# Window attention on one core: where TensorE weighs the values, behind the next pair's maxima or in front of the additions

## The chip, the cores and the metric

One core of a Trainium2 chip runs the whole kernel. The metric is the device time of one execution in microseconds (us), as the median of the runs shown. A core has five engines with a queue of instructions each, which are worked off in order: TensorE (PE, its weight loads are PEld), VectorE (DVE), ScalarE (ACT), GpSimd (POOL) and SyncE (SP, which issues most transfers). They wait for each other by semaphores.

## The reference

x has 8 samples of 32 x 32 positions with 256 channels. Two stages run over it:

```
x = x + attention(groupnorm(x))      # windows of 8 x 8, 16 heads of 16, bias by relative position, shift mask
x = x + lif(groupnorm(x))            # a linear layer, then spikes of leaky neurons over the 8 samples
attention: scores = (q * 0.25) @ k.T + bias + mask ; softmax over the keys ; out = softmax @ v
```

The group norm has 32 groups of 8 channels, with mean and variance over all positions of a sample.

## The kernel before

**Tiling.** The channels lie on the partitions. A sample is four rows of four windows; a row has 256 positions. The attention works on *pairs*: two windows of one row, 64 in all (n from 0 to 63), with k = n mod 8 as place in the sample and p = n mod 2. An even pair is the left half of a row, an odd pair the right half. Every engine runs a function `pair(n, row, k, s)` 64 times, and the order of instructions on each engine is the order in which that function is written; nothing reorders it but the semaphores' waits.

**What one pair needs.** q, k and v of a row are made by TensorE from the normalised row, split into a high and a low part (three products each): `project_q` and `project_k` in odd pairs for the row after next, `project_v` in even pairs for the next row. ScalarE and VectorE copy them out of PSUM as a high and a low half precision part (`q_high`, `k_high`, `v_high`, and `q_low`, `k_low`, `v_low`). SyncE moves q and k into stacks by twelve transfers for a row (`move_q_and_k`). Then, for pair n:

- `max_scores`: TensorE computes the scores once with the queries on the partitions (`max_ps`), VectorE takes the negative maximum over the keys (`maxima`).
- `turn_maxima`: TensorE transposes these, ScalarE copies them to `max_rows` (line 606).
- `scores`: TensorE computes the scores again with the keys on the partitions (`score_ps`, one buffer of two banks): 32 products (line 1023), 8 products that add the biases (line 1032), then a wait for `max_rows`, and 16 products that add the maxima (line 1039). All of these are matmuls on quarters of the array (64 x 64 tiles), four at a time.
- ScalarE takes the exponential twice for each half of the heads, to single precision (`probs`, line 615) and to half precision (`p_hi`, line 616). GpSimd takes the difference (`p_lo`, line 447).
- `weigh_values`: TensorE multiplies the exponentials by the values, 24 matmuls on the full array (line 1065) into `pv_ps`, which has one buffer of two banks. It waits for both halves of `p_lo`, in odd pairs for `v_lo`, and for `attn_done` of the pair before, because VectorE must have read `pv_ps`.
- VectorE divides by the sums (`attention_out`, line 814), TensorE transposes (`turn_attention`, line 1075), ScalarE copies (line 579), GpSimd adds to x (line 433).

The stages overlap: in pair n TensorE computes the scores of n, the maxima of n + 1, the values of n - 1, and turns the attention of n - 2. `project_q` writes the bank that v was in, and so waits until VectorE has read v (`v_lo_done`).

**Norms beside the pairs.** The norm of a later sample is worked out in some pairs (`norm_beside`). Its group means are two small matmuls, `average_means` (line 922, stage 0, pair k = 6, and pair 0), its variances `average_variances` (line 926, stage 1, k = 7; pair 1; pair 60 for the last norm). Both are called from `weigh_values` as `beside`, ahead of its matmuls, and wait for VectorE's moments (line 683) or spreads. VectorE works on the variances (line 704) ahead of dividing the attention. The last norm's roots are GpSimd's, ahead of the `p_lo` of pair 61.

After the pairs, the second stage (LIF) runs over 32 units, one after the other.

Line numbers are those of the kernel before.

Of the kernel before, what the change touches and what calls it, by code (L numbers as in the profile page):

```python
# [6 lines left out]
def swin_attention_then_lif_kernel(nc, image, x, qkv_w, qkv_b, bias_table, lif_w, lif_b, out):  # L7
# [40 lines left out]
    with ctx:  # L48
# [154 lines left out]
        def is_first(n, lag):  # L203

            return isinstance(n, int) and n < lag
# [32 lines left out]
        def is_last_pair(n):  # L238

            return isinstance(n, int) and n == PAIRS - 1  # L240
# [12 lines left out]
        BODY = 2 * WROWS  # L253
# [663 lines left out]
        def _(pe):  # L917
# [6 lines left out]
            def average_variances(norm, width, averages):  # L924
                pe.wait_ge(norm_dve, norm * NORM_STEPS + 4)
                pe.matmul(averages[:, NORMS:NORMS + width], group_avg[:, :], tiny[2][:, 0:width], start=True, stop=True)\
                  .then_inc(norm_pe, 1)
# [84 lines left out]
                                             start=False, stop=(w == 1 and m == 1 and h == 1))  # L1012
                last.then_inc(max_ps_done, 1)

            def scores(n, row, k):

                slot, p = k // 2 % 2, k % 2
                for g, w in itertools.product(range(QUADS), range(2)):
                    col = (2 * g + w) * WS
                    for h, e in itertools.product(range(HALVES), range(2)):  # L1020
                        at = h * WCOLS + 2 * p + w
                        rows = stacks_of[e ^ h]
                        pe.matmul(score_ps[halves[e], h, col:col + WS], k_stack[slot][rows, g, at, :], q_stack[slot][rows, g, at, :],
                                  start=(g == 0 and w == 0), stop=False)
                first, last_variant = variant(k, 0), variant(k, 1)
                for part in range(2):
                    for h, e in itertools.product(range(HALVES), range(2)):
                        rows = halves[e ^ h]
                        biases = bias_s[rows, part, first:last_variant + 1, h, :, :].rearrange("p v g i -> p g v i")
                        if last_variant == first:  # L1030
                            biases = biases.to_broadcast([WS, QUADS, 2, WS])
                        pe.matmul(score_ps[halves[e], h, :].rearrange("p (g w i) -> p g w i", g=QUADS, w=2), flip[rows, :], biases,
                                  start=False, stop=False)
                pe.wait_ge(max_rows_done, n + 1)
                for w, m in itertools.product(range(2), range(2)):
                    for h, e in itertools.product(range(HALVES), range(2)):
                        rows = halves[e ^ h]
                        dst = score_ps[halves[e], h, :].rearrange("p (m q w i) -> p m w q i", m=2, q=2, w=2)[:, m, w, :, :]
                        last = pe.matmul(dst, pick_max[rows, (2 * w + m) * 2 + h, :],  # L1039
                                         max_rows[p][rows, :].rearrange("p (q i) -> p q i", q=2),  # L1040
                                         start=False, stop=(w == 1 and m == 1))
                        if w == 1 and m == 1 and e == 1:
                            last.then_inc(score_ps_done, 1)
# [51 lines left out]
            def pair(n, row, k, s):  # L1095
                p = k % 2
                if p == 0 and not is_last_row(row):
                    project_v((k // 2 + 1) % 2, row + 1)
                elif p == 1 and not is_last_row(row, 2):
                    project_q(k // 2 % 2, row + 2)  # L1100
                    project_k(k // 2 % 2, row + 2, n - 2)
                if is_first(n, 8):
                    pe.wait_ge(bias_lo_done, variant(k, 1) + 1)
                following = (n + 1, row + 1 if p else row, (k + 1) % BODY)

                wait(pe, p_hi_done, n * 2)
                turn_maxima(n)
                scores(n, row, k)
                norm, _, width, stage = norm_beside(s, k)
                beside = None  # L1110
                if stage == 0:
                    beside = lambda: average_means(norm, width, spare_averages)
                if stage == 1:
                    beside = lambda: average_variances(norm, width, spare_averages)
                if not is_last_pair(n):
                    await_max_operands(*following)
                    max_scores(following[2])
                if not is_first(n, 1):
                    weigh_values(n - 1, row if p else row - 1, (k - 1) % BODY, beside)
                elif beside:  # L1120
                    beside()
                if p == 1 and not is_last_row(row, 2):
                    pe.wait_ge(k_lo_done, row + 3)
                if not is_first(n, 2):
                    turn_attention(n - 2, p)
                if is_last_pair(n):
                    unit_products(0, 0)
# [54 lines left out]
```

## Time and profile before

| | us |
|---|---|
| runs shown (3) | 482.02, 482.65, 490.40 |
| median | 482.65 |
| profiled execution, its own time | 487.65 |
| its span, first to last instruction | 485.80 |

| engine | busy us | share of the span |
|---|---|---|
| TensorE matmuls | 412.3 | 85% |
| TensorE weight loads | 346.8 | 71% |
| VectorE | 401.1 | 83% |
| ScalarE | 381.5 | 79% |
| GpSimd | 279.5 | 58% |

The shares are means over a start (to about 85 us), the steady stretch of pairs (to about 390), the last pairs (to about 415) and the second stage. Times in the rows below are us from the first instruction. A row of the timeline has its start, its length, the engine, the line, the operation, what it writes and reads with sizes, how often it stands there merged, and in brackets the idle time of its engine before it with what ended that.

### The profile page before, as it was taken

How to read it: one execution, taken by the hardware profiler on the slowest of the kernel's cores; microseconds unless marked ns; L12 is line 12 of the kernel's file. 1: busy time of each engine (PE TensorE's matmuls, PEld its weight loads, DVE VectorE, ACT ScalarE, POOL GpSimd, SP SyncE). 2: the span in 40 equal slices, each digit the busy share in tenths (PEclk: the TensorE clock that was granted, in tenths of full speed). 3: DMA queues.
4: the chain of work that ended last, by engine and by line, in shares of the span. 5: the costliest groups of instructions: out<-in, count | busy, mean ns of one | idle time of the engine just before them, and what ended most of it. 6: DMA issues, size and time to landing. Idle time of an engine off the chain costs nothing.

```text
span 485.8 us, 22209 instructions
## 1 busy us (share of the span) xinstructions
PE 412.3 (85%) x9320; PEld 346.8 (71%) x9320; DVE 401.1 (83%) x872; ACT 381.5 (79%) x913; POOL 279.5 (58%) x392
## 2 busy tenths in 40 slices
PE   0476768999999999999989997999799886799996
PEld 0465657777777777787777786878677775588885
DVE  6767995998898889889889995988687875689887
ACT  3377897999998889999989995999798866546550
POOL 5625786786667557767866693669565558400000
PEclk9987998999999999999999997999999988899999
DMA  6422221233333232332323323122212220133333
GB/s 210 137 82 72 90 69 61 85 98 97 96 98 94 89 111 92 102 95 94 107 89 98 95 92 104 49 72 68 84 63 74 68 70 3 43 123 124 143 133 131
DMA packets 42488, 44.98 MB, mean 93 GB/s; under 512 B 8082, under 2 KB 33940, under 8 KB 42388
## 3 DMA queue, kind: packets, MB, share of 16 engines
q1 hardware_dynamic: 41632, 43.55, 27.0%
q8 instruction: 74, 1.21, 1.1%
q14 instruction: 26, 0.21, 0.1%
q10 hardware_dynamic: 756, 0.01, 0.1%
HBM read 9.97 MB, written 8.39 MB: 38 GB/s over the span
## 4 chain that ended last, share of the span: by engine, by line
PE 44%; SPq 15%; ACT 14%; DVE 11%; DMA 7%; issue 5%; POOL 3%; ACTq 0%; DVEq 0%; POOLq 0%
SPq L320 15%; PE proj_ps L950 5%; PE pv_ps L1065 5%; DMA k_stack<-k_flat 5%; PE proj_ps L952 4%; PE proj_ps L951 4%; ACT k_flat L514 3%; ACT v_hi L531 3%; PE score_ps L939 3%; PE score_ps L1039 3%; PE proj_ps L939 3%; PE pv_ps L939 3%; PE max_ps L939 2%; DVE v_lo L793 2%; ACT max_rows L606 2%
## 5 line engine op out<-in xcount | busy, mean ns | idle before, releaser
L447 POOL TENSOR_TENSOR p_lo<-probs,p_hi 128x512 f16<-128x512 f32 x128 | 146.5, 1166 | 109.3 <-ACT p_hi L616 87.0
L799 DVE TENSOR_REDUCE neg_max<-max_ps 128x16 f16<-128x1024 f32 x64 | 78.3, 1223 | 20.9 <-PE max_ps L1010 19.9
L615 ACT ACTIVATE probs<-score_ps 128x512 f32<-128x512 f32 x128 | 76.9, 601 | 22.9 <-PE score_ps L1039 18.7
L950 PE MATMUL proj_ps<-xn_hi,w_hi 128*128 128x256 f32 x256 | 79.4, 310 | 17.8 <-POOL xn_lo L400 11.8
L616 ACT ACTIVATE p_hi<-score_ps 128x512 f16<-128x512 f32 x128 | 77.2, 603 | 0.0
L951 PE MATMUL proj_ps<-xn_lo,w_hi 128*128 128x256 f32 x256 | 74.2, 290 | 0.0
L952 PE MATMUL proj_ps<-xn_hi,w_lo 128*128 128x256 f32 x256 | 74.0, 289 | 0.0
L793 DVE TENSOR_TENSOR v_lo<-proj_ps,v_hi 64x256 f16<-64x256 f32 x128 | 54.2, 423 | 20.3 <-ACT v_hi L531 18.8
L950 PEld LDWEIGHTS proj_ps<-xn_hi,w_hi 128*128 128x128 f32 x256 | 51.2, 200 | 23.2 <-issue 16.4
L1065 PE MATMUL pv_ps<-v_hi,p_hi 128*128 128x68 f16 x512 | 56.3, 198 | 3.0 <-POOL p_lo L447 3.0
L531 ACT ACTIVATE v_hi<-proj_ps 64x256 f16<-64x256 f32 x128 | 50.5, 394 | 10.0 <-PE proj_ps L962 8.3
L814 DVE TENSOR_TENSOR attn<-pv_ps,recip 64x256 f32<-64x256 f32 x128 | 54.0, 422 | 3.0
L1065 PE MATMUL pv_ps<-v_lo,p_hi 128*128 128x68 f16 x512 | 56.1, 195 | 0.0
L1065 PE MATMUL pv_ps<-v_hi,p_lo 128*128 128x68 f16 x512 | 55.8, 196 | 0.0
L1065 PEld LDWEIGHTS pv_ps<-v_hi,p_hi 128*128 128x128 f16 x512 | 49.3, 101 | 5.5 <-POOL p_lo L447 3.5
L1039 PEld LDWEIGHTS score_ps<-max_rows,pick_max 64*64 64x64 f16 x1024 | 16.8, 106 | 49.9 <-ACT max_rows L606 49.3
L951 PEld LDWEIGHTS proj_ps<-xn_lo,w_hi 128*128 128x128 f32 x256 | 51.3, 200 | 0.0
L952 PEld LDWEIGHTS proj_ps<-xn_hi,w_lo 128*128 128x128 f32 x256 | 51.2, 200 | 0.0
L433 POOL TENSOR_TENSOR xc<-xc,attn_cm 128x256 f32<-128x256 f32 x64 | 47.2, 738 | 6.5 <-ACT attn_cm L579 6.5
L661 DVE BATCH_NORM_STATS2 x_stats<-xc 128x6 f32<-128x256 f32 x128 | 47.4, 416 | 3.7 <-DMA xc<-in_x_dram 2.7
L579 ACT ACTIVATE attn_cm<-proj_ps,b_cols 128x128 f32<-128x128 f32 x128 | 41.3, 389 | 10.3 <-PE proj_ps L1075 10.2
L1065 PEld LDWEIGHTS pv_ps<-v_lo,p_hi 128*128 128x128 f16 x512 | 49.0, 100 | 0.2 <-issue 0.2
(129 smaller groups left out, 1142.7 us busy)
## 6 DMA issues: line engine op xcount, KB each, us to landing
q_stack<-q_flat SPq DMA_DIRECT2D x192, 64.0 KB
k_stack<-k_flat SPq DMA_DIRECT2D x192, 64.0 KB
xc<-in_x_dram SPq DMA_DIRECT2D x32, 256.0 KB, 3.4
out_dram<-xc SPq DMA_DIRECT2D x32, 256.0 KB, 2.4
w_raw<-in_qkv_w_dram SPq DMA_DIRECT2D x1, 768.0 KB, 6.5
bias_raw<-in_bias_table_dram SPq DMA_DIRECT2D x16, 32.0 KB
w_lif<-in_lif_w_dram SPq DMA_DIRECT2D x1, 256.0 KB, 4.6
b_cols<-in_qkv_b_dram ACTq DMA_DIRECT2D x4, 0.2 KB
```

Source lines behind the costliest of these rows:

```text
L320: sp.dma_start(stacks[slot][first:first + D, :, :, :].rearrange("d g n i -> d g (n i)"), flat[slot][r * WS:(r + 1) * WS, part, :])\
L447: pool.tensor_tensor(p_lo[p][:, quads, :, :].rearrange("p g w i -> p (g w i)"), probs[:, quads, :, :].rearrange("p g w i -> p (g w i)"), p ...
L531: last = act.activation(v_block(v_hi[slot], w, e), v_part(w, e), ACT.Copy)
L615: act.activation(probs[:, quads, :, :].rearrange("p g w i -> p (g w i)"), score_ps[:, h, :], ACT.Exp)
L616: act.activation(p_hi[p][:, quads, :, :].rearrange("p g w i -> p (g w i)"), score_ps[:, h, :], ACT.Exp)\
L793: last = dve.tensor_tensor(v_block(v_lo[slot], w, e), v_part(w, e), v_block(v_hi[slot], w, e), ALU.subtract)
L799: dve.tensor_reduce(neg_max[:, :].rearrange("p (m n) -> p m n", m=2)[:, :, 0:8], max_ps[:, :, :].rearrange("p m (n j) -> p m n j", j=WS), ...
L814: last = dve.tensor_tensor(attn[k % 2][rows, :, :, :], heads[rows, :, w, :, 0:D], recip[rows, :, w, :].unsqueeze(3).to_broadcast([WS, HALV ...
L950: pe.matmul(dst, w_hi[:, c, cols], high[:, tok], start=(c == 0), stop=False)
L951: pe.matmul(dst, w_hi[:, c, cols], low[:, tok], start=False, stop=False)
L952: last = pe.matmul(dst, w_lo[:, c, cols], high[:, tok], start=False, stop=(c == HALVES - 1))
L1065: last = pe.matmul(cols[:, :, g, :], pp[p][:, h * QUADS + g, :, :].rearrange("p w i -> p (w i)"), vv[k // 2][:, p, h * QUADS + g, :, :, :] ...
```

## The change

In even pairs the call of `weigh_values` (or of `beside` alone, where there are no values, as in pair 0) moves into `scores`, between the bias products and the wait for `max_rows`. In odd pairs it stays behind `max_scores`. Nothing else is changed.

```diff
-            def scores(n, row, k):
+            def scores(n, row, k, values=None):
...
                         pe.matmul(score_ps[halves[e], h, :].rearrange("p (g w i) -> p g w i", g=QUADS, w=2), flip[rows, :], biases,
                                   start=False, stop=False)
+                if values:
+                    values()
                 pe.wait_ge(max_rows_done, n + 1)
...
                 turn_maxima(n)
-                scores(n, row, k)
                 norm, _, width, stage = norm_beside(s, k)
                 beside = None
                 if stage == 0:
                     beside = lambda: average_means(norm, width, spare_averages)
                 if stage == 1:
                     beside = lambda: average_variances(norm, width, spare_averages)
+
+                def values():
+                    if not is_first(n, 1):
+                        weigh_values(n - 1, row if p else row - 1, (k - 1) % BODY, beside)
+                    elif beside:
+                        beside()
+
+                scores(n, row, k, None if p else values)
                 if not is_last_pair(n):
                     await_max_operands(*following)
                     max_scores(following[2])
-                if not is_first(n, 1):
-                    weigh_values(n - 1, row if p else row - 1, (k - 1) % BODY, beside)
-                elif beside:
-                    beside()
+                if p:
+                    values()
```

## Rows read from the trace of the kernel before

**Rows 1.** Windows, 85 to 390: us, then busy us (instructions) of each engine, clock.

```profile
85.00:390.00 305.00, 278.82 (x7452) 231.43 (x7452) 262.86 (x581) 273.42 (x666) 207.51 (x266) 0.99 0.28 89
```

**Rows 2.** Waits, 85 to 390: who waited for whom, us, times, longest.

```profile
ACT probs L615 <- PE score_ps L1039: 16.1, 27, 0.9
...
PE max_ps L1003 <- DMA k_stack<-k_flat: 8.1, 10, 2.2
```

**Rows 3.** Timeline of TensorE in pair 18, a plain even pair.

```profile
151.12 0.42 PE L1023 MATMUL score_ps<-q_stack,k_stack 48*64 48x64 f16 x32
151.37 0.63 PE L1032 MATMUL score_ps<-bias_s,flip 64*64 64x512 f16 x8
152.32 0.42 PE L1039 MATMUL score_ps<-max_rows,pick_max 64*64 64x128 f16 x16 [0.31 <-ACT max_rows L606]
...
152.78 0.42 PE L1010 MATMUL max_ps<-k_stack,q_stack 48*64 48x64 f16 x32
153.14 0.20 PE L1065 MATMUL pv_ps<-v_hi,p_hi 128*128 128x68 f16 x1
...
153.90 0.41 PE L1075 MATMUL proj_ps<-ident,attn 128*128 128x128 f32 x2
154.15 0.36 PE L950 MATMUL proj_ps<-xn_hi,w_hi 128*128 128x256 f32 x1
```

**Rows 4.** Timeline of VectorE in pair 18.

```profile
150.86 0.86 DVE L814 TENSOR_TENSOR attn<-pv_ps,recip 64x256 f32<-64x256 f32 x2
...
153.14 0.87 DVE L793 TENSOR_TENSOR v_lo<-proj_ps,v_hi 64x256 f16<-64x256 f32 x2 [0.29 <-ACT v_hi L531]
```

**Rows 5.** Timeline of ScalarE in pair 18: the second copy of v, the exponential.

```profile
152.29 0.81 ACT L531 ACTIVATE v_hi<-proj_ps 64x256 f16<-64x256 f32 x2
153.13 0.60 ACT L615 ACTIVATE probs<-score_ps 128x512 f32<-128x512 f32 x1
```

**Rows 6.** Timeline of all engines in pair 14, with a norm's means.

```profile
128.99 0.39 DVE L683 BATCH_NORM_AGGREGATE moments<-x_stats 128x2 f32<-128x24 f32 x2
...
130.24 0.60 ACT L615 ACTIVATE probs<-score_ps 128x512 f32<-128x512 f32 x1
130.25 0.38 PE L922 MATMUL pv_ps<-moments,group_avg 128*128 128x2 f32 x2
...
130.49 0.19 PE L1065 MATMUL pv_ps<-v_hi,p_hi 128*128 128x68 f16 x1
```

**Rows 7.** Timeline of VectorE and ScalarE in pair 46, with a norm's means.

```profile
312.58 0.39 DVE L683 BATCH_NORM_AGGREGATE moments<-x_stats 128x2 f32<-128x24 f32 x2
...
313.87 0.60 ACT L615 ACTIVATE probs<-score_ps 128x512 f32<-128x512 f32 x1
```

**Rows 8.** Timeline of VectorE and ScalarE in pair 8, after a norm's variances.

```profile
95.21 0.86 DVE L814 TENSOR_TENSOR attn<-pv_ps,recip 64x256 f32<-64x256 f32 x2
...
96.49 0.60 ACT L615 ACTIVATE probs<-score_ps 128x512 f32<-128x512 f32 x1
```

**Rows 9.** Timeline of VectorE and ScalarE in pair 40, after a norm's variances.

```profile
275.07 0.86 DVE L814 TENSOR_TENSOR attn<-pv_ps,recip 64x256 f32<-64x256 f32 x2
...
276.69 0.60 ACT L615 ACTIVATE probs<-score_ps 128x512 f32<-128x512 f32 x1
```

**Rows 10.** Timeline of all engines in pair 0.

```profile
37.96 0.60 ACT L615 ACTIVATE probs<-score_ps 128x512 f32<-128x512 f32 x1
...
39.06 0.39 DVE L683 BATCH_NORM_AGGREGATE moments<-x_stats 128x2 f32<-128x24 f32 x2
...
41.90 0.64 PE L1003 MATMUL max_ps<-bias_q,ident_h 64*64 64x512 f16 x4 [4.19 <-ACT bias_q L541]
...
42.90 0.59 PE L922 MATMUL pv_ps<-moments,group_avg 128*128 128x2 f32 x2
```

**Rows 11.** Timeline of GpSimd (p_lo of pair 61) and ScalarE (pair 62).

```profile
403.98 2.26 POOL L447 TENSOR_TENSOR p_lo<-probs,p_hi 128x512 f16<-128x512 f32 x2
...
405.21 0.60 ACT L615 ACTIVATE probs<-score_ps 128x512 f32<-128x512 f32 x1 [2.76 <-POOL p_lo L447]
```

## The prediction

> **What bounds the kernel now.** I read the busy shares of the stretch in which all pairs look alike, then the list of waits, then single pairs in order of time. In that stretch ScalarE works 273.42 of 305.00 us, nine tenths, VectorE 262.86, and TensorE shows 278.82 of matmuls whose spans overlap [rows 1]. Of ScalarE's 31.6 us of idle time 16.1 lie in 27 waits of 0.60 us each for the additions of the maxima, and these stand in odd pairs, where nothing lies between the copy of the maxima and the exponentials [rows 2]. TensorE in turn waits for the copy of the maxima in front of its additions, 0.31 us in pair 18 [rows 3]: this is the hole that the values would now lie in.
>
> Pair 18 is an even pair without anything special. The products of its scores start at 151.12, the bias products at 151.37; these run until 152.00, and TensorE then stands until the additions at 152.32 [rows 3]. The additions, the next pair's maxima (152.78), the product of values (153.14 to 153.90), the turning of the attention and the projection of q (154.15) follow without a gap [rows 3]. Two rows say who really sets the pace there. The exponential starts at 153.13, 0.81 us after the additions began and not 0.6 as in odd pairs, so it came when ScalarE was done with the second copy of v, not when the scores were done [rows 3, 5]. And v_lo ends on VectorE at 153.14 + 0.87 = 154.01, 0.14 us before q's projection begins: that projection may not overwrite v's bank before it [rows 3, 4]. So in an even pair TensorE's end is tied to v_lo and ScalarE's start to its own queue; an earlier end of TensorE's block has no taker.
>
> **The change part by part.** In the 31 even pairs from 2 on, the 24 matmuls of the values of pair n-1 move in front of the additions of pair n. Their number stays the same, and TensorE's is the only queue in which anything changes place, and no transfer is issued from it. Four waits move with them to the head of TensorE's queue: for p_lo of pair n-1 (GpSimd), for attn of pair n-2 (VectorE, which must have read the bank), in some pairs for the moments of a norm (VectorE) together with the two small matmuls that average them, and, being an in-order queue, all that stood behind: additions, maxima of n+1, the turning, the projection. For the additions wait the exponentials, and with them ScalarE.
>
> *Plain even pairs.* The bias matmuls end at 152.00 by the row; a matmul's row overlaps the next one by about 0.17 (0.20 long at a spacing of 0.03), so TensorE can take new work at about 151.83 [rows 3]. attn of pair 16 is done at 150.86 + 0.86 = 151.72 [rows 4], and a handover of 0.1 (an estimate, under the 0.14 from v_lo to the projection) makes 151.82: just in time. Going from 64x64 tiles to full ones costs something: 32 products of the scores take 0.25 to the next line (151.12 to 151.37), 32 of the same size in front of the values 0.36 (152.78 to 153.14), so I take 0.10 for the switch [rows 3]. For the way back no row stands alone; between 0 and 0.10, I take 0.05. The value block takes 0.76. Additions then begin at 151.83 + 0.10 + 0.76 + 0.05 = 152.74 instead of 152.32, the exponential can start 0.55 later (0.60 of the odd pairs' wait less the handover), 153.29 against 153.13: +0.16. The cover of ScalarE's second v copy swallows the most, not quite all. Maxima of n+1 end some 0.4 later, still before VectorE has done v_lo.
>
> The Trainium skill, in TensorEngine Tiling (Array Packing), Key Properties, says that changing the tiling mode, not just the tile, drains the TensorE. That speaks against this change, since an even pair now goes 64, 128, 64, 128 where it went 64, 128. The row's 0.11 agrees that there is a price, though it shows one direction; if there were none, the plain pairs would cost nothing and the sum would be about 2.5 us less.
>
> Of the 20 or so plain pairs most are followed by some slack (below); I count 1.0 us for all, between 0 and 20 x 0.16 = 3.2.
>
> *Pairs with a norm's means in them* (seventh pair of a sample: 14, 22, 30, 38, 46; pair 6 has ScalarE so late that it costs nothing). VectorE finishes the moments only at 128.99 + 0.39 = 129.38, 0.89 us after pair 14's bias products began; today TensorE asks for them at 130.25, when they are long there [rows 6]. Now: 129.38 + 0.10 handover + 0.24 for the two small matmuls (130.25 to 130.49) + 0.10 + 0.76 + 0.05 + 0.55 = 131.18 for the exponential that started at 130.24: +0.94 [rows 6]. In pair 46, the last, 312.58 + 0.39 + 1.80 = 314.77 against 313.87: +0.90 [rows 7]. Five pairs, 4.6 us.
>
> *Pairs after a norm's variances* (first pair of a sample: 8, 16, 24, 32, 40). VectorE did the variances ahead of attn, which is then late: in pair 8 at 95.21 + 0.86 = 96.07, plus 1.56 (the terms above without the small matmuls) 97.63 against 96.49: +1.14 [rows 8]; in pair 40 275.93 + 1.56 = 277.49 against 276.69: +0.80 [rows 9]. Five pairs between these, 4.9 us.
>
> Together 9.5. ScalarE goes from an even pair's exponentials to the next odd pair's without idle time but the 0.6, so the delay travels on. Where the odd pair then finds TensorE waiting for the moved keys, the delay uses up that wait: there are 10 such waits, 8.1 us, four of them (1.4 us of the 8.1, read along the timeline) behind these ten pairs [rows 2]. For short waits of ScalarE in the odd pairs I take off another 0.9, an estimate whose lower end is nothing. 9.5 - 2.3 = 7.2.
>
> *Pair 0* has no values, but the means of a norm go in front of its additions. Their moments end at 39.06 + 0.39 = 39.45, while the exponential started at 37.96 [rows 10]. 39.45 + 0.10 + 0.45 (the two small matmuls' 0.59 less their tail) + 0.05 + 0.55 = 40.60: +2.6. The maxima of pair 1 wait for a bias table that ScalarE makes behind these exponentials (41.90), so they go with it, and q's projection with them; the means' 0.59 between the two is gone [rows 10]. I take 2.1, between 2.0 and 2.6.
>
> *Pair 62.* GpSimd, held by the last norm's roots, ends p_lo of pair 61 at 403.98 + 2.26 = 406.24 [rows 11]. Today the scores are ready by then and the exponential starts at 405.21, on p_lo's first half [rows 11]. Now the additions stand behind the values, which need both halves: 406.24 + 0.10 + 0.10 + 0.76 + 0.05 + 0.55 = 407.80, +2.6; ScalarE saves about 0.2 of a later wait. 2.4, all of it on the way into the second stage, which nothing shortens.
>
> Sum: 1.0 + 7.2 + 2.1 + 2.4 = 12.7 us. The profiled execution took 487.65 us (span 485.80), so it would be 500.35; the median of the runs shown is 482.65, 5.0 lower, and 12.7 above that is **495.4 us**.
>
> **The rivals.** *TensorE is the bound (faster).* It shows the longest busy time [rows 1] and stands before the additions in nearly every pair. If v_lo did not hold q's projection, an even pair would win the standing time less two switches, 152.32 - 151.83 - 0.15 = 0.34; times 31 that is 10.5 us: 472. Against it stand v_lo's 0.14 and ScalarE's nine tenths. It decides if v_lo is done well before TensorE comes to the projection, which the rows do not show.
> The Trainium skill, in Perfetto Trace Analysis, Identifying the Most-Contended Engine, holds matmul busy time for a poor measure and wants weight loads counted; these are 231.43 us here [rows 1], so by that rule TensorE is not the most contended, as I forecast.
>
> *The queue of moved keys sets the pace (no measurable change).* A row of windows waits for the stacks of q and k, and ScalarE's path is bypassed where that wait ends last. If the ten delays all fall into such waits, outside this one execution or because the transfers start as early as before, only pair 0 and pair 62 remain: 2.1 + 2.4 = 4.5 us, 487.2. For it: ten such waits, of up to 2.2 us [rows 2]. Against: six of the ten pairs have none behind them, and the transfers of a row start after the odd pair's additions, which are themselves late.
>
> *Nothing is absorbed (slower still).* If the waits for keys stay as long as they are, all of 9.5 + 3.2 + 2.1 + 2.6 = 17.4 counts: 500.1.
>
> *No effect*: the waits now at the head are all met in time, as in pair 18, in every pair. The rows of pairs 0, 8, 14 and 62 exclude it for any run in which VectorE keeps its order.
>
> **How the numbers follow.** Two per cent, about what a measurement of this kernel tells from no change, is 9.65 us: 492.3. Chances: forecast 0.60 (its own range 491 to 498, a tenth of it below 492.3), nothing absorbed 0.13, keys set the pace 0.20, TensorE bound 0.04, no effect 0.03. Slower by over 2%: 0.54 + 0.13 = 0.67; within: 0.06 + 0.20 + 0.03 = 0.29; faster: 0.04. The range goes from the keys' 487 to 501, a little above nothing absorbed, for the way back between tile sizes at its upper bound.
>
> **What would show it.** In the profile after: TensorE's wait for the copy of the maxima nearly gone; in its place waits of the value block for attn, moments and, once, p_lo; in pair 18 the exponential within 0.2 us of the end of the second v copy; in pairs like 14 and 8 ScalarE idle for about 0.9 us in front of the exponentials; pair 0's additions at about 40; pair 62's exponential at 2.6 us more behind its p_lo. Wrong would be: q's projection starting clearly earlier behind v's projection, or waits for the keys shrinking by as much as the delays add.

## The result and the profile after

The changed kernel takes 499.19 us (median of four runs, 495.59 to 500.72) against 484.63 for the kernel before beside it (482.02 to 490.4): a ratio of 1.031, with an interval of 1.021 to 1.041. It is slower. The median lies 3.8 us above the forecast and within its range; the difference of the medians is 14.6 us where 12.7 were forecast. The execution that was profiled took 499.86 us with a span of 498.1, which is 12.3 more than the span of before. From L1034 on, line numbers are two higher than in the listing: the additions are now L1041, the values L1067.

Windows of the kernel after, its steady stretch, columns as in [rows 1]:

```profile
85.00:400.00 315.00, 284.93 (x7529) 234.57 (x7530) 267.84 (x583) 274.01 (x672) 210.68 (x271) 0.99 0.27 87
```

I cut the stretch ten us longer than in [rows 1] so that it holds about the same instructions (7529 matmuls for 7452, 672 of ScalarE for 666). ScalarE has worked 274.01 us in it where it had 273.42: what came is waiting. The list of waits of the same stretch (who waited for whom, us, times, longest) shows where:

```profile
ACT probs L615 <- PE score_ps L1041: 30.9, 53, 1.1
PEld score_ps L1041 <- ACT max_rows L606: 19.5, 28, 0.7
...
PEld pv_ps L1067 <- POOL p_lo L447: 6.9, 13, 0.8
...
PE pv_ps L1067 <- DVE attn L814: 4.1, 5, 0.9
PE pv_ps L922 <- DVE moments L683: 4.0, 7, 1.5
...
PE max_ps L1003 <- DMA k_stack<-k_flat: 3.4, 7, 0.8
```

ScalarE waits for the additions 53 times instead of 27, 30.9 us instead of 16.1 [rows 2]: the even pairs have joined the odd ones. Weight loads wait for the copy of the maxima in 28 cases only, 27 of them in odd pairs; in the even pairs the waits for p_lo, attn and the moments have taken its place. The waits of matmuls for the moved keys are down from 8.1 us to 3.4 [rows 2].

Pair 18, the plain even pair, in the timeline of the kernel after:

```profile
156.75 0.86 DVE L814 TENSOR_TENSOR attn<-pv_ps,recip 64x256 f32<-64x256 f32 x2
157.13 0.63 PE L1032 MATMUL score_ps<-bias_s,flip 64*64 64x512 f16 x8
157.76 0.19 PE L1067 MATMUL pv_ps<-v_hi,p_hi 128*128 128x68 f16 x1
158.04 0.81 ACT L531 ACTIVATE v_hi<-proj_ps 64x256 f16<-64x256 f32 x2
158.48 0.19 PE L1067 MATMUL pv_ps<-v_hi,p_lo 128*128 128x68 f16 x1
158.60 0.42 PE L1041 MATMUL score_ps<-max_rows,pick_max 64*64 64x128 f16 x16
158.88 0.87 DVE L793 TENSOR_TENSOR v_lo<-proj_ps,v_hi 64x256 f16<-64x256 f32 x2 [0.28 <-ACT v_hi L531]
159.14 0.60 ACT L615 ACTIVATE probs<-score_ps 128x512 f32<-128x512 f32 x1 [0.29 <-PE score_ps L1041]
159.90 0.35 PE L950 MATMUL proj_ps<-xn_hi,w_hi 128*128 128x256 f32 x1
```

The additions start 1.47 us after the bias products where it was 0.95 [rows 3]; the second copy of v ends at 158.85, and ScalarE now stands for 0.29 us where the copy used to hide the additions [rows 5]. v_lo still ends 0.15 before q's projection begins (159.75, 159.90), as before: the end of TensorE's block was not brought forward.

The special pairs in the same timeline: pair 0 (from 37.96), pair 8 (97.86), pair 14 (133.49), pair 26 (204.58) and pair 62 (413.37):

```profile
37.96 0.39 DVE L683 BATCH_NORM_AGGREGATE moments<-x_stats 128x2 f32<-128x24 f32 x2
38.40 0.58 PE L922 MATMUL pv_ps<-moments,group_avg 128*128 128x2 f32 x2 [2.01 <-DVE moments L683]
39.59 0.60 ACT L615 ACTIVATE probs<-score_ps 128x512 f32<-128x512 f32 x1 [2.50 <-PE score_ps L1041]
...
97.86 1.16 DVE L704 TENSOR_SCALAR root_guess<-tiny 128x2 int32<-128x2 int32 x1
...
99.30 0.86 DVE L814 TENSOR_TENSOR attn<-pv_ps,recip 64x256 f32<-64x256 f32 x2
100.31 0.19 PE L1067 MATMUL pv_ps<-v_hi,p_hi 128*128 128x68 f16 x1 [0.85 <-DVE attn L814]
101.68 0.60 ACT L615 ACTIVATE probs<-score_ps 128x512 f32<-128x512 f32 x1 [1.14 <-PE score_ps L1041]
...
133.49 0.39 DVE L683 BATCH_NORM_AGGREGATE moments<-x_stats 128x2 f32<-128x24 f32 x2
134.02 0.35 PE L922 MATMUL pv_ps<-moments,group_avg 128*128 128x2 f32 x2 [0.41 <-DVE moments L683]
135.61 0.60 ACT L615 ACTIVATE probs<-score_ps 128x512 f32<-128x512 f32 x1 [0.87 <-PE score_ps L1041]
...
204.58 0.20 PE L1067 MATMUL pv_ps<-v_hi,p_hi 128*128 128x68 f16 x1 [0.30 <-POOL p_lo L447]
205.97 0.60 ACT L615 ACTIVATE probs<-score_ps 128x512 f32<-128x512 f32 x1 [0.56 <-PE score_ps L1041]
...
413.37 2.26 POOL L447 TENSOR_TENSOR p_lo<-probs,p_hi 128x512 f16<-128x512 f32 x2
415.69 0.24 PE L1067 MATMUL pv_ps<-v_hi,p_hi 128*128 128x68 f16 x1 [3.44 <-POOL p_lo L447]
417.15 0.64 PE L1041 MATMUL score_ps<-max_rows,pick_max 64*64 64x128 f16 x16
417.91 0.60 ACT L615 ACTIVATE probs<-score_ps 128x512 f32<-128x512 f32 x1 [6.06 <-PE score_ps L1041]
```

In each of them TensorE's first value (or average) names the engine that it waited for, and ScalarE's first exponential names the additions: the chain that was forecast. Two distances are new. In pair 26 p_lo is late, which no term of the sum had. In pair 62 the additions begin 1.46 us after the first value, where pair 18 needs 0.84; its value block runs at half the clock (windows, below).

### The profile page after: what moved, and what is told of

Read it like the earlier page. It is cut to its first block, busy times and chain, and to the rows that moved or that the text cites. A ratio compares the mean times of both kernels' runs of the same rounds, so it can differ in the third digit from the quotient of the medians.

```text
span 498.1 us, 22209 instructions
## 1 busy us (share of the span) xinstructions
PE 418.3 (84%) x9320; PEld 348.6 (70%) x9320; DVE 404.9 (81%) x872; ACT 379.1 (76%) x913; POOL 279.1 (56%) x392
## 4 chain that ended last, share of the span: by engine, by line
PE 38%; DVE 14%; ACT 14%; SPq 12%; issue 8%; POOL 8%; DMA 5%; ACTq 0%; DVEq 0%; POOLq 0%
SPq L320 12%; PE pv_ps L1067 6%; POOL p_lo L447 4%; DMA k_stack<-k_flat 4%; ACT p_hi L616 3%; PE score_ps L1041 3%; PE proj_ps L950 3%; PE score_ps L939 3%; ACT k_flat L514 3%; PE proj_ps L939 3%; PE pv_ps L939 3%; DVE x_stats L661 3%; PE proj_ps L952 2%; PE proj_ps L951 2%; PE max_ps L939 2%
## 5 line engine op out<-in xcount | busy, mean ns | idle before, releaser
L950 PE MATMUL proj_ps<-xn_hi,w_hi 128*128 128x256 f32 x256 | 80.7, 315 | 27.3 <-DVE w_lo L752 8.7
L1067 PEld LDWEIGHTS pv_ps<-v_hi,p_hi 128*128 128x128 f16 x512 | 49.4, 101 | 21.8 <-POOL p_lo L447 11.7
L1067 PE MATMUL pv_ps<-v_hi,p_hi 128*128 128x68 f16 x512 | 56.0, 197 | 9.8 <-DVE attn L814 5.1
L1067 PE MATMUL pv_ps<-v_lo,p_hi 128*128 128x68 f16 x512 | 55.8, 195 | 0.0
L1067 PE MATMUL pv_ps<-v_hi,p_lo 128*128 128x68 f16 x512 | 55.5, 196 | 0.0
L1067 PEld LDWEIGHTS pv_ps<-v_hi,p_lo 128*128 128x128 f16 x512 | 49.0, 98 | 0.0
L1067 PEld LDWEIGHTS pv_ps<-v_lo,p_hi 128*128 128x128 f16 x512 | 48.9, 100 | 0.0
L492 ACT ACTIVATE unit<-xc,shift,rstd 128x256 f32<-128x256 f32 x64 | 34.0, 594 | 16.0 <-PE score_ps L939 8.1
```

The lines of the kernel that those rows point to most:

```text
L950: pe.matmul(dst, w_hi[:, c, cols], high[:, tok], start=(c == 0), stop=False)
L1067: last = pe.matmul(cols[:, :, g, :], pp[p][:, h * QUADS + g, :, :].rearrange("p w i -> p (w i)"), vv[k // 2][:, p, h * QUADS + g, :, :, :] ...
```

## The experiments

**Theory**: the values, and what they wait for, put off the additions; ScalarE's exponentials then start later than its second copy of v would let them, and the delay goes through to the end. **Rival 1**: TensorE is the bound, and the two further switches of tile size per even pair are what costs. **Rival 2**: the waits themselves cost, at whichever place they lock an engine. **Rival 3**: only the norm pairs, or only pairs 0 and 62, carry the loss. Later runs ask whether the waiting can be bought back.

The table is worked out along the timelines: the mean time from the turning of the maxima to the first exponential of the pair, in us, by position of the pair in its sample (first, seventh, third, fifth pair), then the waits of weight loads for moved keys in pairs 9 to 59 (they begin earlier than the matmuls' waits of [rows 2] and are longer), the steady stretch from pair 9's first exponential to pair 57's, and the span of the profiled execution. Each line is one execution.

```
kernel             first  seventh  third  fifth  keys  steady  span
before             2.06   2.08     2.08   2.06   10.4  274.0   485.8
after              3.13   2.93     2.49   2.30    5.0  277.5   498.1
values_second      2.05   2.07     2.08   2.07   10.5  271.6   484.1
waits_only         2.14   2.07     2.09   2.07   10.2  273.0   483.5
plain_only         2.06   2.07     2.49   2.29    8.0  274.2   485.3
norms_only         3.17   2.93     2.09   2.12    7.0  275.2   487.4
norms_root_means   2.42   2.30     2.08   2.06    6.9  271.8   483.2
ends_only          2.05   2.07     2.08   2.10   10.0  273.0   490.0
ends_behind        3.15   2.93     2.48   2.29    4.0  277.2   493.1
mended             2.34   2.30     2.47   2.26    8.6  275.5   489.9
before_again       2.06   2.07     2.08   2.07   10.4  274.0   487.5
```

TensorE's granted clock was 0.5 for some us of the steady stretch in before, before_again, waits_only, plain_only and ends_only, and 1.0 throughout in the other six. Of those, values_second has pairs like those of before; so its 271.6 us is the fair measure for the steady stretch of the others among the six.

**values_second.** The values go one step back, behind the additions but still in front of the next maxima. The number of switches per pair stays that of the change.

```diff
-                scores(n, row, k, None if p else values)
+                scores(n, row, k)
+                if not p:
+                    values()
```

> In even pairs the additions stay first and the values come right behind them, ahead of the next pair's maxima: as many changes of tile size as in the changed kernel, but no wait and no work in front of the additions. Theory (the cost is the exponentials' delay by what now stands in front of the additions; ScalarE's queue sets the pace): the loss is gone, 0 to +1 per cent against the kernel before, and pair 62 costs nothing. Rival (the values' earlier place costs TensorE itself, by the two further switches between tile sizes and by waits at the head of its queue): most of the changed kernel's +3 per cent stays. If TensorE were the bound, nothing is won either, as it still stands for the copy of the maxima.

Measured: 1.003 (0.999 to 1.008). The loss is gone. Its pair 18 in the timeline:

```profile
152.03 0.81 ACT L531 ACTIVATE v_hi<-proj_ps 64x256 f16<-64x256 f32 x2
152.06 0.42 PE L1041 MATMUL score_ps<-max_rows,pick_max 64*64 64x128 f16 x16 [0.31 <-ACT max_rows L606]
...
152.41 0.20 PE L1067 MATMUL pv_ps<-v_hi,p_hi 128*128 128x68 f16 x1
...
152.87 0.60 ACT L615 ACTIVATE probs<-score_ps 128x512 f32<-128x512 f32 x1
```

The exponential again follows the copy of v without idle time. Rival 1 falls as to its price: the extra switches cost nothing that is seen. Whether TensorE is the bound is left to q_short, since TensorE still stands for the copy of the maxima here. What costs is the place of the values, with their waits, ahead of the additions.

**waits_only.** Only the waits of the values (for p_lo, attn and the norm's step) go in front of the additions, in the even pairs from 2 to 60; the matmuls stay where they were.

```diff
+                def waits():
+                    pe.wait_ge(p_lo_done, n * 2)
+                    wait(pe, attn_done, n - 1)
+                    if stage in (0, 1):
+                        pe.wait_ge(norm_dve, norm * NORM_STEPS + (1, 4)[stage])
...
-                scores(n, row, k, None if p else values)
+                scores(n, row, k, waits if p == 0 and 0 < n < 62 else None)
...
-                if p:
-                    values()
+                values()
```

> TensorE's order of matmuls as in the kernel before, but in the 30 even pairs between the ends the value block's waits (for p_lo, attention and, where there is a norm, moments) stand in front of the wait for the copy of the maxima, without its matmuls. Theory (a wait and the 0.8 us of work behind it exceed the 0.8 us by which ScalarE is late only together): pairs like 8 lose 0.2 to 0.3 us, all others nothing, the waits for keys take it up: ratio 1.00 to 1.003. Rival (the waits alone are the price): +5 to +7 us, 1.010 to 1.015.

Measured: 0.999 (0.994 to 1.003). Pair 8 in its timeline, the pair with the latest attn:

```profile
96.33 0.42 PE L1041 MATMUL score_ps<-max_rows,pick_max 64*64 64x128 f16 x16 [0.80 <-DVE attn L814]
...
96.86 0.60 ACT L615 ACTIVATE probs<-score_ps 128x512 f32<-128x512 f32 x1 [0.23 <-PE score_ps L1041]
```

TensorE waits 0.80 us for attn, and the exponential is 0.23 late, because the copy of v covers the rest; the mean of the first pairs rises by 0.08. So the waits alone fall too (rival 2). In the same pairs wait and block together cost 2.8 per cent (ends_behind, below), and wait and block behind the additions cost nothing that is seen (values_second). The block ahead of the additions without any wait was not run; the nearest to it are pairs whose waits are met almost in time, such as the fifth ones, which are 0.24 us late.

**plain_only, norms_only, ends_only.** The change in one class of pairs each; elsewhere the values stay behind.

```diff
-                scores(n, row, k, None if p else values)
+                front = k in (2, 4) and n < 60
+                scores(n, row, k, values if front else None)
...
-                if p:
+                if not front:
                     values()
```

In norms_only the condition is `k in (0, 6) and 8 <= n < 48`, in ends_only `n in (0, 62)`.

> The values in front of the additions only in the 15 even pairs without a norm's wait and away from both ends (third and fifth pair of each sample but the last's fifth). Theory: each of these pairs delays its exponentials by 0.2 us, or 0.5 in the third pair of a sample where p_lo is late; 5.4 us in sum, of which the waits for moved keys take more than half: +1 to +4 us, ratio 1.00 to 1.01. Rival (every pair pays alike by its order): 15 of 31 pairs, +7 us, ratio 1.015.

> The values in front of the additions only in the ten pairs 8, 14, 16, 22, ... 46 that stand beside or behind a norm's steps on VectorE. Theory: 0.9 us each in front of the exponentials, 9 us in sum, of which waits for moved keys take 1.5 to 3: +6 to +7.5 us, ratio 1.012 to 1.016. Rival (every pair pays alike): 10 of 31 pairs, +4 us, ratio 1.008; rival (the keys' queue sets the pace): +0 to +2 us.

> The values (in pair 0 the means) in front only in pairs 0 and 62. Theory: 2.0 to 2.9 us for pair 0 and 3.4 for pair 62, all on the path: ratio 1.011 to 1.013. Rival (the run with both put back gained less, so what follows takes most of it up): 1.00 to 1.005.

Measured: 1.012 (1.000 to 1.023), 1.016 (1.004 to 1.029) and 1.015 (1.007 to 1.024). The table says that plain pairs and norm pairs behave alone as they do in the whole change, to within 0.05 us; the way from the turning to the exponential in pair 62 is 6.61 us in ends_only as in the whole change (3.31 before). In each class the exponentials are late, which ends rival 3 as to the mechanism; as to the time, the interval of the plain pairs only just leaves out 1 (1.0004). The parts do not add up: the three ratios make 4.3 per cent where the whole has 3.1, and the spans of the three profiles only 5.3 us where the whole has 12.3. The intervals are 1.7 to 2.5 per cent wide, so these runs settle the mechanism in each pair but not its share of the time. The end in ends_only, GpSimd and ScalarE in the timeline:

```profile
405.25 2.26 POOL L447 TENSOR_TENSOR p_lo<-probs,p_hi 128x512 f16<-128x512 f32 x2
...
409.80 0.60 ACT L615 ACTIVATE probs<-score_ps 128x512 f32<-128x512 f32 x1 [6.06 <-PE score_ps L1041]
```

The exponential comes 409.80 - 407.51 = 2.29 us after p_lo, in the whole change 417.91 - 415.63 = 2.28, and in the kernel before it came 1.03 ahead of it [rows 11].

**ends_behind.** The complement: the change in all even pairs but 0 and 62 (`front = p == 0 and 0 < n < 62`).

> The changed kernel with pairs 0 and 62 put back to the order before. Theory: pair 0 gave 1.6 us and pair 62 3.4 us in the trace, both on the path; the sum of 5 us goes, ratio 1.018 to 1.023 where the changed kernel has 1.031. Rival (the ends' delays are taken up by the second stage or by what follows): stays at 1.03.

Measured: 1.028 (1.021 to 1.035), more than expected. In its trace pair 62 is as before (3.33 us from the turning to the exponential, 6.61 in the whole change, 3.31 before), and the way from pair 57's exponential to pair 63's is 33.53 us as against 37.34 in the change and 33.50 before. So 3.8 us are back at the end of the first stage, yet the ratio fell by 0.3 points only, well within its interval. The spans of the profiles do fit: ends_behind has 7.3 us more than before, ends_only 4.2, together 11.5 of the 12.3. Its start is as slow as the change's: 57.03 us from pair 1's exponential to pair 9's (56.73 in the change, 53.61 before).

**norms_root_means.** norms_only, with two things mended: the small matmuls for the means go behind the maxima again, and VectorE makes the roots' guess behind attn, not ahead of it.

```diff
-                        weigh_values(n - 1, row if p else row - 1, (k - 1) % BODY, beside)
+                        weigh_values(n - 1, row if p else row - 1, (k - 1) % BODY, beside if not front else None)
...
                 if not front:
                     values()
+                elif beside:
+                    beside()
...
+                if stage == 1:
+                    norm_guess(norm, width)
```

> The values in front only in the same ten pairs 8, 14, 16, ... 46 as in the run with these alone (ratio 1.016), but with what made them late moved out of the way: the small matmuls of the means stand behind the next maxima again, and VectorE makes the first guess of the roots behind the attention instead of ahead of it. Theory (the waits for moments and for a late attention are the price): each of the ten pairs falls from 0.9 us to 0.2 to 0.4, so +0 to +2 us, ratio 1.00 to 1.004. Rival (the place of the values itself is the price): unchanged at about 1.016.

Measured: 1.007 (1.004 to 1.011). VectorE in its pair 8:

```profile
94.86 0.86 DVE L817 TENSOR_TENSOR attn<-pv_ps,recip 64x256 f32<-64x256 f32 x2
95.75 0.56 DVE L706 TENSOR_SCALAR root_guess<-tiny 128x2 int32<-128x2 int32 x1
```

attn now comes first. The delay of the first pairs falls from 1.1 to 0.36 us and that of the seventh from 0.85 to 0.22, so both named causes are real. The steady stretch, 3.6 us over values_second in norms_only, hardly differs from it here; the ratio falls from 1.016 to 1.007, though the two intervals overlap. What is left of the delay has the size of a plain pair's, which I read as the value block itself.

**mended.** Both cures in all even pairs but 0 and 62.

> The changed kernel with pairs 0 and 62 as before, the small matmuls of the means behind the next maxima, and VectorE's first guess of the roots behind the attention: the values of 30 even pairs still stand in front of the additions, but the long waits are gone. Theory: 0.2 to 0.4 us is left for each pair, 8 us in sum, of which the waits for keys take 5, and up to 2 us for the clock at the start: ratio 1.005 to 1.012. Rival (the place of the values itself): stays at 1.02 to 1.03.

Measured: 1.017 (1.008 to 1.025), half a point above what was expected. The even pairs are late by 0.2 to 0.4 us each, as the table says, which costs 3.9 us of the steady stretch against values_second. Another 2.1 us are lost between pairs 2 and 3 (10.42 us against 8.33 in the kernel before). That the guess for a norm's roots now stands behind pair 1's attn does not explain them: norms_root_means has it there too and takes 8.40 us. TensorE's clock does (windows, columns as in [rows 1]):

```profile
57.20:64.00 6.80, 6.04 (x64) 5.84 (x68) 3.81 (x8) 3.80 (x11) 4.50 (x11) 0.50 0.22 68
```

The kernel before, in the profile of before_again, has the clock at 0.50 in the same projection and takes 9.84 us from pair 2 to pair 3, with nothing changed. No form of the change that keeps the values ahead of the additions beat the kernel before.

**q_short**, on the kernel before: q is projected from the high parts alone; the matmuls of the low parts are left out. If TensorE sets the pace, this must give time back.

```diff
-                project_channels(banks[6], 0, xn_hi[slot], xn_lo[slot]).then_inc(q_ps_done, 1)
+                for h in range(HALVES):
+                    for c in range(HALVES):
+                        last = pe.matmul(banks[6][:, h * ROWTOK:(h + 1) * ROWTOK], w_hi[:, c, h * 128:(h + 1) * 128],
+                                         xn_hi[slot][:, c * ROWTOK:(c + 1) * ROWTOK], start=(c == 0), stop=(c == HALVES - 1))
+                last.then_inc(q_ps_done, 1)
```

> The kernel before, its order unchanged, with q projected from the high parts alone (4 matmuls instead of 12 for a row; the low parts of q's projection are left out): TensorE has 8 x 0.117 = 0.94 us less work in each of 30 odd pairs. Theory (ScalarE's queue and the keys' transfers set the pace, TensorE's end is tied to others): 0 to -1 per cent. Rival (TensorE is the bound): -28 us, -6 per cent.

Measured: 0.988 (0.983 to 0.993). The waits of its steady stretch (85 to 395):

```profile
PEld proj_ps L950 <- ACT attn_cm L579: 26.2, 27, 1.1
...
ACT probs L615 <- PE score_ps L1043: 16.1, 27, 0.9
```

The same wait for attn_cm has 2.3 us in the kernel before. Most of what TensorE saves (0.94 us in each of 30 pairs), it now waits for ScalarE, and ScalarE's own wait is to the tenth what it was.

**xn_in_hole and v_early_xn**, on the kernel before, ask the opposite: whether filling ScalarE's 0.6 us in the odd pairs gives time back. xn_in_hole moves the high part of xn there; v_early_xn also moves v's projection to right behind the odd pairs' additions.

```diff
-                if p == 0 and not is_first(n, 1) and not is_last_row(row, 2):
-                    xn_high(k // 2 % 2, row + 3)
...
                     .then_inc(max_rows_done, 1)
+                if p == 1 and not is_last_row(row, 3):
+                    xn_high(nxt % 2, row + 4)
... (v_early_xn alone)
-                if p == 0 and not is_last_row(row):
-                    project_v((k // 2 + 1) % 2, row + 1)
+                if n == 0:
+                    project_v(1, 1)
...
+                if p == 1 and not is_last_row(row, 2):
+                    project_v(k // 2 % 2, row + 2)
```

> The kernel before with TensorE's order unchanged; ScalarE makes the high part of the normalised row in odd pairs between the copy of the maxima and the exponentials, where it stands idle for 0.6 us, instead of at the start of the next even pair (0.5 to 0.65 us). If ScalarE's queue alone sets the pace: 30 x 0.5 = -15 us, ratio 0.97. If ScalarE then waits for v's projection instead, which it does already in 13 even pairs of the stretch, and the keys' transfers hold their share: -2 to -6 us, ratio 0.988 to 0.996. If TensorE is the bound: 1.00.

> The same, and TensorE projects v in odd pairs right behind the additions of the maxima, not behind the turning of the attention at the start of the next even pair. Then neither the wait for moved keys nor the values stand in front of v's projection, and ScalarE finds v when it comes. Theory (ScalarE's queue is the bound, with v's projection and the keys next): -8 to -15 us, ratio 0.97 to 0.985, as the keys' wait is now filled with work. Rival (the later maxima of the next pair delay VectorE and the turned maxima by the projection's 1.5 us): no gain or up to +2 per cent.

Measured: 1.005 (1.000 to 1.009) and 1.057 (1.045 to 1.069). Both theories of ScalarE's queue missed; the first came out at what was written for TensorE as the bound. The waits of xn_in_hole, 85 to 395:

```profile
ACT v_hi L531 <- PE proj_ps L962: 16.1, 27, 1.2
...
ACT probs L615 <- PE score_ps L1039: 0.6, 1, 0.6
```

15.5 of the 16.1 us are filled, and 10.6 us open again one step on: the wait for v's projection was 5.5 us before. So at that step ScalarE waits for TensorE's order of work; that TensorE's amount of work is not the bound, q_short had shown. The steady stretch of this one profile is 268.2 us, 3.4 less than that of values_second, but the whole runs are not faster. Bringing that projection forward opened a third one, in v_early_xn's waits:

```profile
DVE neg_max L799 <- PE max_ps L1010: 51.3, 26, 2.1
...
ACT attn_cm L579 <- PE proj_ps L1075: 35.2, 28, 1.8
```

16.4 and 8.4 before. So ScalarE is not a bound in the sense that any idle time taken from it comes back. I read the pair as a closed loop through three engines, in which ScalarE's path is the longest way round by little.

**before_again.** One further profile of the kernel before, to see whether its long waits for keys belong to one execution.

> The kernel before once more, for one look: whether its two long waits for moved keys (2.4 us in pair 43, 2.1 us in pair 51) and the fall of TensorE's clock to its lower level behind the first belong to the kernel or to the one execution that was profiled. If to the execution: the waits for keys between pairs 9 and 59 fall from 10.7 us to 6 to 8, and the span from pair 9's to pair 57's exponential from 274.0 to about 270.

Measured: a span of 487.5 us, 10.4 us of waits for keys in pairs 9 to 59, and the same 274.0 us from pair 9 to pair 57. The longest stands at the same pair, here in the timeline of TensorE:

```profile
296.13 0.41 PE L1003 MATMUL max_ps<-bias_q,ident_h 64*64 64x512 f16 x4 [1.61 <-DMA k_stack<-k_flat]
```

In the first profile it has 2.20 us, at 295.50. These waits belong to the kernel and not to one execution. The fall of the clock behind the longest recurs as well, for a shorter stretch (0.51 from 296.90 to 300.40), and a further one to 0.50 from 344.70, where the first profile has 1.00. At the start the two executions of the one kernel differ by 1.5 us: from pair 1's exponential to pair 9's they take 53.61 and 55.09.

## Why the prediction came out as it did

**The mechanism held**, and each step of it can be seen. TensorE's wait for the copy of the maxima went in the even pairs, nothing took the time that was freed (v_lo holds q's projection by 0.15 us, as it did), and the exponentials wait for the additions. By the Trainium skill (Perfetto Trace Analysis, Identifying the Most-Contended Engine), TensorE's headroom is judged by its weight loads and the work done, not by matmul spans. q_short agrees, since fewer matmuls gave 1.2 per cent and mostly a wait.

**Plain pairs.** Forecast +0.16; measured +0.24 in fifth pairs, +0.41 in third ones, and +0.25 in pair 18, so that its exponential missed the 0.2 us behind the copy of v that were to show the forecast right. The value block starts 0.63 us after the bias products and not 0.56, being held by attn or p_lo, which end at 157.61 and 157.62. The way back from full tiles to 64x64 is 158.60 - 158.48 - 0.03 = 0.09, near the upper end of what I allowed. In third pairs GpSimd's p_lo comes late, as in pair 26: I had taken this wait to be met everywhere but in pair 62. By the Trainium skill, in TensorEngine Tiling (Array Packing), Key Properties, a change of tiling mode drains the TensorE. The rows agree that a change has a price, about 0.1 us each way, and in values_second it costs nothing that is seen where nobody waits behind it.

**Norm pairs.** In pair 14 the exponential comes 135.61 - 133.88 = 1.73 us after the moments (forecast 1.80), in pair 8 101.68 - 100.16 = 1.52 after attn (forecast 1.56). The means over five pairs are +0.85 and +1.07, within the forecast's 0.90 to 0.94 and 0.80 to 1.14 or just below. norms_root_means confirms both causes by taking them away. Pair 2, behind pair 1's variances, is of this kind too (late by 1.27 us); I had counted it with the plain ones.

**What was absorbed** is the first mis-sized term. I took off 1.4 us for waits for keys behind ten pairs, out of 8.1. In the two profiles these waits fell by 8.1 - 3.4 = 4.7 us, since plain pairs too run into them (in plain_only the weight loads' waits fall from 10.4 to 8.0). The delays themselves are larger too: from pair 10 to pair 56 the exponentials of the even pairs are late by 13.1 us in all, of which the nine norm pairs have 8.5, as forecast, and the plain ones 4.6, where I had counted 1.0 and at most 3.2. From pair 9's exponential to pair 57's the kernel lost only 3.55 us, where the forecast's parts for this stretch make about 7. A part of that is not the change's: in the kernel before, TensorE had half the clock around pair 43, which the kernel after lacks (windows of before; columns as in [rows 1]):

```profile
73.00:76.40 3.40, 3.40 (x18) 3.40 (x17) 1.06 (x3) 1.56 (x4) 2.00 (x3) 0.50 0.25 69
...
294.80:301.70 6.90, 6.21 (x114) 5.63 (x118) 2.99 (x6) 2.68 (x7) 4.24 (x4) 0.51 0.32 106
```

I read about 3 us of the stretch's difference from that second window, and this reading is an estimate. Against values_second, whose clock does not fall there, the kernel after lost 277.5 - 271.6 = 5.9 us; measured so, the net forecast of 7 is near, by two terms that were both too small and cancel.

**Pair 0** was sized well as a delay: the exponential comes 39.59 - 38.35 = 1.24 us after the moments (forecast 1.15), where it came 1.49 ahead of them before. Up to pair 1's exponential the kernel lost 1.8 us of span where I took 2.1, but this is not set apart from the start's own changes: runs with pair 0 as before reach that point anywhere from 48.58 us (plain_only) to 51.32 (ends_behind), the kernel after at 50.85.

**Pair 62** is the second mis-sized term: 2.28 us behind p_lo instead of 1.56, so 3.3 instead of 2.6, and 3.8 instead of 2.4 up to pair 63. The step that failed is the 0.76 for the value block with the 0.55 behind it: both were taken at the full clock. Windows of the kernel after:

```profile
72.10:78.90 6.80, 4.86 (x22) 4.86 (x23) 3.83 (x8) 4.32 (x12) 4.74 (x5) 0.50 0.21 60
...
89.10:92.50 3.40, 3.18 (x15) 3.19 (x16) 3.20 (x9) 2.00 (x6) 3.10 (x4) 0.51 0.41 128
413.40:423.60 10.20, 7.05 (x162) 5.23 (x163) 3.09 (x6) 4.88 (x12) 5.87 (x7) 0.50 0.02 4
```

From 413.40 on TensorE has 0.50 of its clock, the 1.2 GHz level. That lies within a stand of 3.44 us (412.25 to 415.69) in which it waited for p_lo.

**The start** is a term that was missing. From pair 1's exponential to pair 9's the kernel lost 3.1 us, of which pair 8's delay explains about one. Projections of pairs 4 to 7 run at 0.50 and 0.51 in two windows of together 10.2 us, where the kernel before has one of 3.4: pairs 4 to 5 take 0.67 us more, 6 to 7 take 1.52 more. How much of this is the change's is not shown. The kernel before itself takes 53.61 us in one profile and 55.09 in the other, in which the clock is low in one more place (windows of before_again):

```profile
58.00:61.40 3.40, 3.35 (x16) 3.38 (x17) 2.26 (x4) 1.30 (x4) 3.09 (x8) 0.50 0.37 109
```

Against the one the loss is 3.1 us, against the other 1.6. ends_behind has the same two windows as the change and takes 57.03 us; values_second, plain_only and norms_only take 53.55 to 53.89. That would fit a loss which comes with the values ahead in all of these pairs together, but with one profile each, and so large a difference between two profiles of one kernel, it is only argued.

So the stages make 1.8 + 3.1 + 3.55 + 3.8 + 0.0 (second stage) = 12.3 us, close to the forecast's 12.7, but by errors that cancel, which is luck: against this one profile of before the middle was put too high, start and end too low.

**The rivals.** TensorE as the bound is refuted by the sign of the change (472 us were due) and by q_short (1.2 per cent where 6 were due); values_second takes away the switches as the price. That the keys' queue takes up everything is refuted as it was put (1.031), though the queue took more than three times what I gave it. No effect is refuted. The rival that nothing is absorbed had 500.1 us, and by the number alone the measured 499.19 is nearer to it than to the forecast; its condition, waits for keys as long as they were, is not met (8.1 to 3.4 us).

**Open** stays why the parts don't add up in time: ends_only costs 1.5 per cent, and its complement is only 0.3 points better than the whole. Pair 62's 3.8 us should make 0.8 points; the intervals of the two (1.021 to 1.041 and 1.021 to 1.035) leave room for that, and the spans of the profiles, 4.2 and 7.3 of 12.3 us, fit it. Low clock at other places in every execution is one reason why the spans of single profiles need not add up; no further run tells the shares apart.

## What to carry to other kernels

Work that is pulled into an engine's waiting time on an in-order queue brings its own waits along and puts off all that stood behind; ask first how late the next engine would have started anyway, since only what goes beyond that cover is paid (here, in the same pairs, the waits alone ahead of the additions 0.999, waits and block 1.028; waits and block one step later, behind the additions, 1.003). Walk that sum for each class of pairs, with the latest producer in each, and at the clock that the engine has there after it has stood. And an engine's idle time is worth filling only if the loop that it lies in gets shorter: here two thirds of a filled hole of 16 us opened again one step on.

## What the runs showed of the hardware

TensorE's granted clock fell from 1.0 to 0.5, from the 2.4 to the 1.2 GHz level, inside a busy kernel, and it fell at other places in other orders of the work, and in part at other places in a second execution of the same kernel. In the kernel before, ahead of the stretch from 294.80, TensorE had stood for the keys (windows):

```profile
292.00:294.80 2.80, 1.06 (x48) 0.42 (x35) 1.35 (x4) 1.94 (x6) 0.00 (x0) 1.00 0.51 149
```

It was busy for 1.06 of 2.80 us. The kernel after has shorter waits for the keys and keeps its clock there, but at its start, ahead of 72.10, it shows the same picture, 1.08 of 2.10 us:

```profile
70.00:72.10 2.10, 1.08 (x54) 0.70 (x46) 2.00 (x6) 2.06 (x6) 2.04 (x4) 0.99 0.30 98
```

Such a wait is not always followed by a fall. In values_second TensorE stands 2.45 us for the same keys, less busy than above, and the clock stays at 1.00, in this window and in the 6.9 us after it:

```profile
292.70:295.50 2.80, 0.37 (x16) 0.21 (x16) 0.64 (x2) 2.03 (x4) 0.81 (x1) 1.00 0.50 140
```

And the wait at the next such place, 1.94 us up to 343.58 in the kernel before and 1.86 up to 343.67 in before_again, left the clock at 1.00 in the first and was followed by 0.50 in the second. So a wait of about two us on TensorE can be paid a second time in the work that follows it, in one execution and not in another, and a change that moves TensorE's gaps can move the places of the low clock with them, in either direction. I had given neither a term in the sum.
